# Cross-attention ahead of a product-key expert layer: 32-row and 32-column matmuls for scores and values, a transposed copy of x, softmax divided before the values, setup in one block with the attention

## The chip, the cores and the metric

The kernel runs on one core of one Trainium2 chip. The metric is the device time of one launch in microseconds (us), as the median of three runs; the profile is one further execution of the same program. The core has five engines with instruction queues of their own: TensorE (PE, matmuls; its weight loads are listed apart as PEld), VectorE (DVE), ScalarE (ACT), GpSimd (POOL) and SyncE (SP, which here only starts transfers).

## The reference, cut

```python
def _L0_xattn_ref(query, key, value, mask, wq, bq, wk, bk, wv, bv, wo, bo):   # H = 16, HD = 32
    q = query @ wq + bq; k = key @ wk + bk; v = value @ wv + bv
    score = jnp.einsum('bhqd,bhkd->bhqk', q, k) / jnp.sqrt(jnp.float32(HD))
    score = score + (1.0 - mask) * -1000000000.0
    alpha = jax.nn.softmax(score, axis=-1)
    context = jnp.einsum('bhqk,bhkd->bhqd', alpha, v)
    return context.transpose(0, 2, 1, 3).reshape(b, -1, D) @ wo + bo
...
x = x + _L0_xattn_ref(_layernorm(x), ctx_1024, ctx_1024, mask_Bx1x1xS2_ff1, ...)
x = x + _L0_ffn_ref(_layernorm(x), w_q, bn_gamma, bn_beta, keys, down_embed, up_embed)
```

x is 2 x 2048 x 512 in fp32, the context 2 x 77 x 512, so that each of 4096 tokens has 16 heads of 77 scores. The second line is a product-key layer: queries are normalised over the batch, the 8 best of 128 keys are taken twice for each of 8 heads, 64 rows of two tables of 16384 x 512 are fetched for each token, and they are weighted with gelu and softmax. Everything is fp32.

## The kernel before, in words

The tokens are 32 tiles (`NT`) of 128 (`P`), 16 to a batch. The program has three blocks, each ended by all engines.

`setup_block` loads the weights and makes what all tiles share: the keys, projected, as `kbd`, a matrix for each batch with the four heads of a group of 128 rows on its diagonal (`GK` = 308 columns for each of four groups, `KC`), and the values as `v_pack`, which holds for each of ten chunks of 128 (head, token) pairs (`NCH`) the 96 columns (`VW`) of the three heads that it can touch, with zeros elsewhere.

`attention_block` runs a pipeline over the tiles. In step s, TensorE works for tile s (it turns the normalised x, `turn_x`, projects the queries in four parts, `project`, and multiplies with `kbd`, `score`), for tile s-2 (it turns the exponentials into `probT`, `turn_prob`, multiplies with `v_pack`, `values`, and turns the sum, `turn_attention`) and for tile s-3 (`output`, the product with wo). `values` begins with a matmul of zeros that opens the whole bank. VectorE adds the mask and takes and subtracts the maximum (`shift_scores`), sums the exponentials (`sum_exp`), divides what the values gave (`norm_attention`), scales q (`scale_q`), normalises x (`norm_x`), and adds the residual with its statistics (`residual`). ScalarE takes one Exp over all 1232 scores and copies what TensorE turned out of PSUM. GpSimd makes the reciprocal roots, adds bo to a second load of x, and normalises x2. When the last tile's scores are done, `second_moments` (x2 transposed times x2, for the batch normalisation) fills TensorE for the rest of the block. What sets the order is the code: each engine's `step` is written out by hand, with semaphores between them.

`expert_block` makes the normalised scoring matrix and then, for each tile, fetches 64 rows for each token with indirect transfers (line 809), takes dot products on VectorE and ScalarE (lines 990 and 1173) and sums weighted rows on TensorE (line 1354).

An fp32 matmul stands in the trace as two records of TensorE, each with a weight load of its own; a transpose is one record. So the 16 matmuls of `project` for a tile are 32 records.

## Time and profile before

| | |
|---|---|
| median of three runs | 3672.28 us (3667.19 to 3675.46) |
| profiled execution, its own time | 3638.82 us |
| its span, first to last instruction | 3637.0 us |
| mean granted clock of TensorE | 0.919 |
| TensorE matmul, VectorE, ScalarE, GpSimd busy | 83%, 67%, 47%, 59% |
| end of the setup block | 27.0 us |
| end of the attention block | about 562 us |

The busy shares are means over three unlike stages. The setup and the attention take the first 562 us, the preparation of the experts some 130 us more, and the rest of the span is the loop over the experts' rows. The profiled execution was 33 us faster than the median of the runs.

### The profile page before, as it was taken

The page shows a single profiled execution, that of the slowest core. Times are in us where ns is not written, and L with a number is a line of the kernel's source. Part 1 is how long each engine was busy: PE and PEld are TensorE (multiplying, and loading weights), DVE is VectorE, ACT ScalarE, POOL GpSimd, SP SyncE. Part 2 cuts the span into 40 slices and gives each one's busy share as a digit, 9 for nine tenths or more (in the row PEclk, how much of TensorE's full clock was granted, in tenths as well). Part 3 has the DMA queues.
Part 4 walks back from the last instruction along what each step waited for, and adds up shares of the span by engine and source line. Part 5 has one row for each costly group of instructions (what it writes and reads, how often), then busy time and mean ns, then how long its engine had stood idle before and what let it go on. Part 6 is the DMA issues. An engine that isn't in the chain of part 4 may idle for free.

```text
span 3637.0 us, 33429 instructions
## 1 busy us (share of the span) xinstructions
PE 3004.5 (83%) x8862; PEld 1495.1 (41%) x8862; DVE 2429.0 (67%) x5214; ACT 1722.7 (47%) x5109; POOL 2134.2 (59%) x2225
## 2 busy tenths in 40 slices
PE   8999999787877877778888878878887877788777
PEld 6787866333333333333333333333333333333333
DVE  5777725576766766667766766667666666666665
ACT  1222201455554555555555555555554555555555
POOL 1343421466666666666666666666666666666665
PEclk9999999899999999988999989989998999999989
DMA  5111101799999999999999999999999999999997
GB/s 191 52 61 52 58 18 55 275 366 368 368 367 364 369 368 368 372 365 362 368 365 371 368 369 375 368 361 362 370 366 366 380 361 366 368 368 361 364 374 306
DMA packets 324684, 1132.59 MB, mean 311 GB/s; under 512 B 36187, under 2 KB 36827, under 8 KB 323880
## 3 DMA queue, kind: packets, MB, share of 16 engines
q0 software_dynamic: 294912, 1073.87, 77.1%
q1 hardware_dynamic: 28800, 55.92, 4.4%
q10 hardware_dynamic: 808, 0.99, 0.1%
q8 instruction: 56, 0.92, 0.1%
q14 instruction: 108, 0.88, 0.1%
HBM read 1113.87 MB, written 16.78 MB: 311 GB/s over the span
## 4 chain that ended last, share of the span: by engine, by line
ACT 23%; another core or an unknown queue 17%; DVE 16%; PE 14%; issue 14%; DVEq 0%; ACTq 0%
ACT rows L1173 16%; PE banks L1354 9%; DVE rows L990 5%; PE banks L1333 3%; DVE expert_diag L1004 3%; ACT expert_act_h L1185 2%; ACT expert_more_rows L1173 2%; DVE expert_top_s L905 2%; DVE expert_top_i L913 1%; PE banks L1268 1%; ACT L1185 1%; DVE expert_best_i L936 1%; DVE expert_coef L996 1%; ACT L1168 1%
## 5 line engine op out<-in xcount | busy, mean ns | idle before, releaser
L809 POOL DMA_INDIRECT rows<-in_table,expert_idx x1824 | 1729.2, 948 | 952.3 <-issue 642.4
L1354 PE MATMUL banks<-rows,expert_diag 128*128 128x512 f32 x3648 | 1753.2, 630 | 494.7 <-DVE expert_diag L1004 310.4
L1173 ACT ACTIVATE rows<-rows 128x512 f32<-128x512 f32 x1824 | 1123.7, 617 | 749.9 <-DVE expert_coef L996 386.6
L1354 PEld LDWEIGHTS banks<-rows,expert_diag 128*128 128x128 f32 x3648 | 719.5, 202 | 1482.2 <-issue 1010.8
L990 DVE TENSOR_TENSOR rows<-rows,banks 128x2048 f32<-128x2048 f32 x456 | 1037.2, 2275 | 11.9 <-issue 6.9
L996 DVE TENSOR_TENSOR expert_coef<-expert_act_h,expert_prob 128x4 f32<-128x4 f32 x512 | 80.6, 157 | 848.7 <-remote 500.6
L1333 PE MATMUL banks<-amat,expert_xnT 128*128 128x512 f32 x992 | 466.1, 592 | 7.8 <-issue 5.8
L1004 DVE TENSOR_TENSOR expert_diag<-banks,expert_coef 128x512 f32<-128x512 f32 x512 | 346.6, 677 | 29.5 <-remote 15.7
L1173 ACT ACTIVATION_READ_ACCUMULATOR rows<-rows 128x1 f32 x1824 | 340.5, 187 | 0.3
L1185 ACT ACTIVATE expert_act_h<-expert_hid 128x4 f32<-128x4 f32 x512 | 105.2, 205 | 437.5 <-remote 339.7
L1354 PE MATMUL banks<-expert_more_rows,expert_diag 128*128 128x512 f32 x448 | 225.7, 650 | 80.5 <-DVE expert_diag L1004 41.8
L1333 PEld LDWEIGHTS banks<-amat,expert_xnT 128*128 128x128 f32 x992 | 188.3, 190 | 243.4 <-issue 239.8
L809 POOL DMA_INDIRECT expert_more_rows<-in_table,expert_idx x224 | 212.1, 947 | 121.3 <-issue 88.6
L1173 ACT ACTIVATE expert_more_rows<-expert_more_rows 128x512 f32<-128x512 f32 x224 | 138.1, 617 | 84.6 <-DVE expert_coef L996 43.9
L1354 PEld LDWEIGHTS banks<-expert_more_rows,expert_diag 128*128 128x128 f32 x448 | 91.3, 209 | 208.2 <-issue 140.6
L373 POOL TENSOR_TENSOR rstd<-attention_var_eps,minus_half 128x1 f32<-128x1 f32 x32 | 17.9, 560 | 246.7 <-DVE attention_var_eps L460 246.7
L913 DVE FIND_INDEX8 expert_top_i<-expert_top_s,banks 128x8 uint32<-128x128 f32 x512 | 139.4, 288 | 20.5 <-issue 20.2
L586 PE MATMUL banks<-attention_xnT,amat 128*128 128x128 f32 x1024 | 137.3, 279 | 2.1 <-ACT attention_xnT L524 2.1
L586 PEld LDWEIGHTS banks<-attention_xnT,amat 128*128 128x128 f32 x1024 | 128.3, 194 | 16.8 <-issue 13.9
L990 DVE TENSOR_TENSOR expert_more_rows<-expert_more_rows,banks 128x2048 f32<-128x2048 f32 x56 | 127.4, 2275 | 0.8 <-issue 0.8
L905 DVE MAX8 expert_top_s<-banks 128x8 f32<-128x128 f32 x512 | 113.1, 282 | 9.8 <-PE banks L1333 8.0
L552 PE MATMUL banks<-amat,attention_attT 128*128 128x512 f32 x256 | 115.2, 592 | 0.0
(133 smaller groups left out, 2227.2 us busy)
## 6 DMA issues: line engine op xcount, KB each, us to landing
rows<-in_table,expert_idx POOLq DMA_INDIRECT x1824
x_t<-in_x SPq DMA_DIRECT2D x32, 256.0 KB, 2.9
attention_xr_t<-in_x SPq DMA_DIRECT2D x32, 256.0 KB, 2.8
x_dram<-rows SPq DMA_DIRECT2D x32, 256.0 KB, 2.0
expert_x_t<-x_dram SPq DMA_DIRECT2D x32, 256.0 KB
out_y<-expert_x_t SPq DMA_DIRECT2D x32, 256.0 KB
rows<-in_w_q SPq DMA_DIRECT2D x4, 1024.0 KB, 6.3
rows<-in_w_qT SPq DMA_DIRECT2D x4, 1024.0 KB, 8.5
```

Source lines behind the costliest of these rows:

```text
L552: mm = pe.matmul(att_ps[:, :], attT[:, c, :], attn_w[:, 1, c, :], start=(c == 0), stop=(c == KC - 1))
L586: mm = pe.matmul(q_ps[:, j, :], attn_w[:, 0, c, j * P:(j + 1) * P], xnT[:, c, :], start=(c == 0), stop=(c == KC - 1))
L809: pool.indirect_dma_start(four(n)[:, k, :], None, table[:, :], bass.IndirectOffsetOnAxis(ap=idx[:, t % 2, at:at + 1], axis=0))\
L905: ins = dve.max(top_s[:, m * TOP:(m + 1) * TOP], score_ps[:, q % 2, i * NK:(i + 1) * NK])
L913: ins = dve.max_index(top_i[:, h // HH, m % 2, h % HH, :], top_s[:, m * TOP:(m + 1) * TOP], score_ps[:, q % 2, i * NK:(i + 1) * NK])
L990: return dve.tensor_tensor(down, down, xn_ps[:, par, :].unsqueeze(1).to_broadcast([P, HALF, D]), ALU.mult)
L996: dve.tensor_tensor(coef[:, j % RING, :], act_h[:, j % RING, :], prob[:, par, j * HALF:(j + 1) * HALF], ALU.mult)\
L1004: dve.tensor_tensor(diag[:, j % RING, :, :], ident_ps.unsqueeze(1).to_broadcast([P, HALF, P]), coef[:, j % RING, :].unsqueeze(2).to_broadc ...
L1173: ins = act.activation(down, down, ACT.Copy, accum_out=hid[:, j % RING, k:k + 1])
L1185: act.activation(act_h[:, j % RING, :], hid[:, j % RING, :], ACT.Gelu_apprx_tanh)\
L1333: mm = pe.matmul(score_ps[:, q % 2, :], xnT[:, par, c, :], amat[:, c, q * 512:(q + 1) * 512], start=False, stop=(c == KC - 1), skip_group_ ...
L1354: mm = pe.matmul(out_ps[:, par, :], diag[:, j % RING, k, :], four(t * HALVES + j)[:, k, D:2 * D], start=(j == 0 and k == 0), stop=(j == HA ...
```

## The change

It touches the first two blocks and one input; `expert_block` is the same text. Setup and attention become one block. The host also hands over x transposed by tile (`x_T`), so that x is neither normalised nor turned ahead of the projection: the mean is taken out of wq once (`centre`), and the reciprocal root of the variance multiplies the scores instead. The bias of q becomes a bias of the scores (`score_bias`, made once for each batch, with the mask in it). Scores are 16 matmuls of 32 rows (one for each head, `scores_of`), and those of the heads r, r+4, r+8, r+12 lie in bank r. Values are 25 matmuls whose stationary side is 32 columns of `v_pack` and whose moving side is a chunk of `probT`; head h writes rows 32 (h mod 4) and following, so the result is already turned. For that, the softmax is divided before it is turned (`normalize`, in two halves), and the maximum is subtracted as the bias of 16 Exp instructions, one for each head. `output` is cut in two around `score`. All loops are written out.

```diff
+            def load_xT(t):
+                wait(sp, "q_done", t - XT_RING + 1)
+                sp.dma_start(xT_t[:, t % XT_RING], x_T[t]).then_inc(xT_in[t % XT_RING], 16)
...
-            def shift_scores(m, par, batch):
...
-                wait(dve, "probT_turned", (m - 1) * NG)
...
-                for i, (h0, n) in enumerate(SCORE_HEADS):
-                    ins = dve.tensor_tensor(
-                        prob[:, par, h0:h0 + n, :],
-                        score_ps[:, i, 0:n * SK].rearrange("p (h k) -> p h k", h=n),
-                        mb.unsqueeze(1).to_broadcast([P, n, SK]), ALU.add)
-                ins.then_inc(ev["masked"], 1)
-                wait(dve, "masked", m + 1)
-                dve.tensor_reduce(smax[:, :], prob[:, par], AX.X, ALU.max).then_inc(ev["max_done"], 1)
-                wait(dve, "max_done", m + 1)
-                dve.tensor_tensor(prob[:, par], prob[:, par],
-                                  smax[:, :].unsqueeze(2).to_broadcast([P, H, SK]),
-                                  ALU.subtract).then_inc(ev["shifted"], 1)
...
+            def mask_scores(t):
+                b = t // TPB
+                to, bias = by_row(prob[:, t % 2]), by_row(score_bias[b])
+                dve.wait_ge(ev["score_done"], t + 1)
+                dve.wait_ge(ev["rstd_done"], t + 1)
+                dve.wait_ge(ev["bias_kept"], (b + 1) * G)
+                wait(dve, "probT_turned", (t - 1) * NG)
+                for r in range(G):
+                    dve.scalar_tensor_tensor(out=to[r], in0=score_bank(0, r), scalar=rstd[:, t:t + 1],
+                                             in1=bias[r], op0=ALU.mult, op1=ALU.add)\
+                       .then_inc(ev["masked"], 1)
+                dve.wait_ge(ev["masked"], (t + 1) * G)
+                dve.tensor_reduce(neg_max[:, t % 2, :], prob[:, t % 2], AX.X, ALU.max, negate=True)\
+                   .then_inc(ev["max_done"], 1)
+            def normalize(t, half):
+                n = 2 * t + half
+                some = slice(half * H // 2, (half + 1) * H // 2)
+                dve.wait_ge(ev["exp_done"], n + 1)
+                dve.tensor_reduce(ssum[:, t % 2, some], prob[:, t % 2, some], AX.X, ALU.add)\
+                   .then_inc(ev["sum_done"], 1)
+                dve.wait_ge(ev["sum_done"], n + 1)
+                dve.reciprocal(rsum[:, t % 2, some], ssum[:, t % 2, some]).then_inc(ev["rsum_done"], 1)
+                dve.wait_ge(ev["rsum_done"], n + 1)
+                dve.tensor_tensor(prob[:, t % 2, some], prob[:, t % 2, some],
+                                  rsum[:, t % 2, some].unsqueeze(2).to_broadcast([P, H // 2, SK]),
+                                  ALU.mult).then_inc(ev["normed"], 1)
...
+            def exps(t, heads):
+                for h in heads:
+                    ins = act.activation(prob[:, t % 2, h, :], prob[:, t % 2, h, :], ACT.Exp,
+                                         bias=neg_max[:, t % 2, h:h + 1])
+                    if h % (H // 2) == H // 2 - 1:
+                        ins.then_inc(ev["exp_done"], 1)
...
+            def copy_attT(b):
+                act.wait_ge(ev["att_part"], (b + 1) * NG)
+                wait(act, "wo_done", b)
+                act.activation(attT[:, :, :], att_ps, ACT.Copy).then_inc(ev["attT_done"], 1)
...
+            for s in range(NT + 1):
+                now, back = s < NT, s >= 1
+                if back:
                     copy_probT(s - 1, 0)
-            pipeline(act, step)
+                    copy_probT(s - 1, 1)
+                if now:
+                    act.wait_ge(ev["max_done"], s + 1)
+                    exps(s, range(0, 8))
+                if back:
+                    copy_probT(s - 1, 2)
+                if now:
+                    exps(s, range(8, 12))
+                if back:
+                    copy_attT(s - 1)
+                if now:
+                    exps(s, range(12, 14))
+                if s + 1 < NT:
+                    copy_qT(s + 1)
+                if now:
+                    exps(s, range(14, 16))
...
-            def turn_x(t):
-                wait(pe, "xn_done", t + 1)
-                wait(pe, "attT_done", t - 2)
-                for c in range(KC):
-                    mm = pe.transpose(turn_ps[:, c, :], xn_t[:, c * P:(c + 1) * P], ident[:, :])
-                mm.then_inc(ev["xn_turned"], 1)
...
+            def scores_of(first, queries, b):
+                for g in range(KC):
+                    for r in range(G):
+                        rows = slice(r * HD, (r + 1) * HD)
+                        mm = pe.matmul(score_bank(first, r)[:, g, :], queries[rows, g, :],
+                                       k_sb[rows, g, b * SK:(b + 1) * SK], start=True, stop=True)
+                return mm
+            def project(t, js):
+                for j in js:
+                    if j == 0:
+                        pe.wait_ge(xT_in[t % XT_RING], (t // XT_RING + 1) * 16)
+                        wait(pe, "masked", (t - 1) * G + 1)
+                    for c in range(KC):
+                        mm = pe.matmul(banks[:, Q_BANK, j * P:(j + 1) * P],
+                                       attn_w[:, 0, c, j * P:(j + 1) * P], xT_t[:, t % XT_RING, c, :],
+                                       start=(c == 0), stop=(c == KC - 1))
+                    if j == KC - 1:
+                        mm.then_inc(ev["q_done"], 1)
+            def score(t):
+                pe.wait_ge(ev["qT_done"], t + 1)
+                wait(pe, "masked", t * G)
+                scores_of(0, qT, t // TPB).then_inc(ev["score_done"], 1)
...
-            def values(b, r, batch):
+            def values(b, r):
 
                 if r == 0:
-                    if isinstance(b, int) and b == 0:
-                        wait(pe, "zeros_made", 1)
+                    wait(pe, "attT_done", b)
+                pe.wait_ge(ev["probT_done"], b * NG + r + 1)
+                pairs = [(c, h) for c in CHUNK_GROUPS[r] for h in range(H)
+                         if h * SK < (c + 1) * P and (h + 1) * SK > c * P]
+                for c, h in pairs:
+                    g, q = divmod(h, G)
+                    at = (h - FIRST_HEAD[c]) * HD
+                    mm = pe.matmul(att_ps[q * HD:(q + 1) * HD, g, :],
+                                   v_pack[:, b // TPB, c, at:at + HD],
+                                   probT[:, r, c % 4 * P:(c % 4 + 1) * P],
+                                   start=(c == h * SK // P), stop=(c == ((h + 1) * SK - 1) // P))
+                mm.then_inc(ev["att_part"], 1)
+            def output(b, cs):
+                if 0 in cs:
+                    pe.wait_ge(ev["attT_done"], b + 1)
                     wait(pe, "x2_done", b)
-                    pe.matmul(att_ps[:, :], zeros[:, 0:P], zeros[:, :], start=True, stop=False)
-                wait(pe, "probT_done", b * NG + r + 1)
-                for i, c in enumerate(CHUNK_GROUPS[r]):
-                    head0 = FIRST_HEAD[c] * HD
-                    mm = pe.matmul(att_ps[:, head0:head0 + VW], probT[:, r, i * P:(i + 1) * P],
-                                   v_pack[:, batch, c, :],
-                                   start=False, stop=(c == NCH - 1))
-                mm.then_inc(ev["att_part"], 1)
...
-            def score(t, batch):
-                wait(pe, "qT_done", t + 1)
-                wait(pe, "masked", t)
-                for i, (h0, n) in enumerate(SCORE_HEADS):
-                    h = h0
-                    while h < h0 + n:
-                        g, stop = h // G, min(h0 + n, (h // G + 1) * G)
-                        mm = pe.matmul(score_ps[:, i, (h - h0) * SK:(stop - h0) * SK], qT[:, g, :],
-                                       kbd[batch][:, g, (h - g * G) * SK:(stop - g * G) * SK],
-                                       start=True, stop=True)
-                        h = stop
-                mm.then_inc(ev["score_done"], 1)
...
-            def step(s, par, half, has, batch):
-                draining = isinstance(s, int) and s >= NT
-                now, back2 = 0 in has, -2 in has
-                if now:
-                    turn_x(s)
-                if -3 in has:
-                    output(s - 3)
-                if now:
-                    project(s, 0)
-                if back2:
-                    turn_prob(s - 2, par, 1)
-                if now:
-                    project(s, 1)
-                if back2:
-                    values(s - 2, 0, batch(-2))
-                    turn_prob(s - 2, par, 2)
-                if now:
-                    project(s, 2)
-                if back2:
-                    values(s - 2, 1, batch(-2))
-                    values(s - 2, 2, batch(-2))
-                if now:
-                    project(s, 3)
-                if draining and s < NT + 2:
-                    second_moments(2, first=(s == NT))
-                if back2:
-                    turn_attention(s - 2)
-                if draining and s < NT + 2:
-                    second_moments(2)
-                if -1 in has:
-                    turn_prob(s - 1, 1 - par, 0)
...
+                                   ctx_sb[:, c, :], start=(c == 0), stop=(c == KC - 1))
+                mm.then_inc(ev["k_made"], 1)
+            pe.wait_ge(ev["centre_made"], 1)
+            pe.wait_ge(wq_in, 16)
+            for c in range(KC):
+                mm = pe.matmul(banks[:, Q_BANK, :], centre[:, :], attn_w[:, 0, c, :],
+                               start=(c == 0), stop=(c == KC - 1))
+            mm.then_inc(ev["mean_made"], 1)
+            pe.wait_ge(ev["bq_spread"], 1)
+            pe.wait_ge(ev["k_biased"], KC)
+            scores_of(4, bq_wide, 0).then_inc(ev["bias_done"], 1)
+            pe.wait_ge(ev["centred"], KC)
+            project(0, range(KC))
+            score(0)
+            pe.wait_ge(ev["bias_kept"], G)
+            scores_of(4, bq_wide, 1).then_inc(ev["bias_done"], 1)
+            setup_values()
+            for s in range(NT + 2):
+                if s >= 2:
+                    output(s - 2, (2, 3))
+                if s == NT:
+                    second_moments(3)
+                if 1 <= s <= NT:
+                    if s == 1:
+                        pe.wait_ge(ev["pad_made"], 1)
+                        pe.wait_ge(ev["pack_kept"], len(PACK_BANKS))
...
+                    turn_prob(s - 1, 1)
+                if s + 1 < NT:
+                    project(s + 1, (0, 1, 2))
+                if s in (NT - 1, NT):
+                    second_moments(1)
+                if 1 <= s <= NT:
+                    turn_prob(s - 1, 2)
+                    for r in range(NG):
+                        values(s - 1, r)
+                if s + 1 < NT:
+                    project(s + 1, (3,))
+                if s in (NT - 1, NT):
+                    second_moments(1)
+                if 1 <= s <= NT:
+                    output(s - 1, (0, 1))
+                if s + 1 < NT:
+                    score(s + 1)
             second_moments(len(moments_left) - 1)
...
```

TensorE's own order shows what stands in one step of a tile. Here are the last twelve of the sixteen pieces of one step before, from after `output` to the scores; L546 `turn_x` (4 transposes) and L552 `output` (4 matmuls) stand ahead of them. L586 is `project`, L562 `turn_prob`, L572 the zeros, L576 `values`, L594 `turn_attention`, L605 `score`; the numbers are those of the output and the count.

```order
L586 MATMUL banks<-attention_xnT,amat 128x128 x4
L562 MATMUL banks<-ident,attention_prob_pad 128x128 x4
L586 MATMUL banks<-attention_xnT,amat 128x128 x4
L572 MATMUL banks<-attention_zeros 128x512
L576 MATMUL banks<-amat,attention_probT 128x96 x4
L562 MATMUL banks<-ident,attention_prob_pad 128x128 x2
L586 MATMUL banks<-attention_xnT,amat 128x128 x4
L576 MATMUL banks<-amat,attention_probT 128x96 x6
L586 MATMUL banks<-attention_xnT,amat 128x128 x4
L594 MATMUL banks<-ident,attention_att 128x128 x4
L562 MATMUL banks<-ident,attention_prob_pad 128x128 x4
L605 MATMUL banks<-bias_row,attention_qT 128x308
```

After that row come two of 128x154 and two more of 128x308, the rest of `score`. And a whole step of the changed kernel, in which L510 is `turn_prob`, L495 `project`, L524 `values`, L535 `output`, L485 `scores_of`.

```order
L510 MATMUL banks<-ident,attention_prob_pad 128x128 x8
L495 MATMUL banks<-attention_xT_t,amat 128x128 x12
L510 MATMUL banks<-ident,attention_prob_pad 128x128 x2
L524 MATMUL banks<-attention_probT,amat 32x128 x25
L495 MATMUL banks<-attention_xT_t,amat 128x128 x4
L535 MATMUL banks<-amat 128x512 x2
L485 MATMUL banks<-bias_row 128x77 x16
L535 MATMUL banks<-amat 128x512 x2
```

The two groups of four transposes (x and the attention) and the matmul of zeros are gone; ten matmuls of 96 columns are 25 with 32 columns of weights, and five of 154 or 308 columns are 16 of 77.

ScalarE before, in one step (L524 copies the turned x, L527 is Exp, L516 and L534 are copies of `probT` and `attT`):

```order
L524 ACTIVATE attention_xnT<-banks 128x512
L527 ACTIVATE attention_prob_pad<-attention_prob_pad 128x1232
L516 ACTIVATE attention_probT<-banks 128x512
L516 ACTIVATE attention_probT<-banks 128x256
L534 ACTIVATE attention_attT<-banks 128x512
L516 ACTIVATE attention_probT<-banks 128x512
```

And after (L433 is Exp of one head, L442 and L448 the same two copies, L428 the copy of the queries, which VectorE made before):

```order
L442 ACTIVATE attention_probT<-banks 128x512 x2
L433 ACTIVATE attention_prob_pad<-attention_prob_pad,attention_neg_max 128x77 x8
L442 ACTIVATE attention_probT<-banks 128x256
L433 ACTIVATE attention_prob_pad<-attention_prob_pad,attention_neg_max 128x77 x4
L448 ACTIVATE amat<-banks 128x512
L433 ACTIVATE attention_prob_pad<-attention_prob_pad,attention_neg_max 128x77 x2
L428 ACTIVATE bias_row<-banks 128x512
L433 ACTIVATE attention_prob_pad<-attention_prob_pad,attention_neg_max 128x77 x2
```

The last two heads' Exp now stands behind the copy of the next tile's queries, which waits for TensorE.

## Rows read from the trace of the kernel before

**Rows 1.** The page's first part: engine, busy us, share of the span, instructions.

```profile
PE 3004.5 (83%) x8862; PEld 1495.1 (41%) x8862; DVE 2429.0 (67%) x5214; ACT 1722.7 (47%) x5109; POOL 2134.2 (59%) x2225
```

**Rows 2.** Busy time by stretch: from:to, length, engines, granted clock, DMA share, GB/s.

```profile
200.00:300.00 100.00, 100.00 (x643) 79.84 (x642) 77.28 (x129) 27.55 (x44) 41.23 (x37) 1.00 0.17 56
...
690.00:3637.00 2947.00, 2364.78 (x5168) 1006.70 (x5168) 2009.80 (x4356) 1571.63 (x4846) 1906.93 (x2012) 0.91 0.95 364
```

**Rows 3.** TensorE's instructions over one step: start us, length us, engine, line.

```profile
259.58 0.60 PE L546 MATMUL banks<-ident,attention_xn_t 128*128 128x128 f32 x4
260.02 3.60 PE L552 MATMUL banks<-amat,attention_attT 128*128 128x512 f32 x8
263.45 1.05 PE L586 MATMUL banks<-attention_xnT,amat 128*128 128x128 f32 x8
264.34 0.60 PE L562 MATMUL banks<-ident,attention_prob_pad 128*128 128x128 f32 x4
264.78 1.06 PE L586 MATMUL banks<-attention_xnT,amat 128*128 128x128 f32 x8
265.77 0.38 PE L572 MATMUL banks<-attention_zeros 1*128 1x512 bf16 x1
266.08 1.13 PE L576 MATMUL banks<-amat,attention_probT 128*128 128x96 f32 x8
267.05 0.38 PE L562 MATMUL banks<-ident,attention_prob_pad 128*128 128x128 f32 x2
267.27 1.06 PE L586 MATMUL banks<-attention_xnT,amat 128*128 128x128 f32 x8
268.16 1.48 PE L576 MATMUL banks<-amat,attention_probT 128*128 128x96 f32 x12
269.48 1.08 PE L586 MATMUL banks<-attention_xnT,amat 128*128 128x128 f32 x8
270.42 0.66 PE L594 MATMUL banks<-ident,attention_att 128*128 128x128 f32 x4
270.92 0.60 PE L562 MATMUL banks<-ident,attention_prob_pad 128*128 128x128 f32 x4
271.35 2.34 PE L605 MATMUL banks<-amat,attention_qT 128*128 128x308 f32 x10
273.53 0.60 PE L546 MATMUL banks<-ident,attention_xn_t 128*128 128x128 f32 x4
```

**Rows 4.** TensorE's weight loads in the first 60 us, grouped: busy us, mean ns.

```profile
L219 PEld LDWEIGHTS setup_k_ps<-setup_v_sb,setup_repeat 77*128 77x128 f32 x40 | 4.6, 192 | 0.5 <-issue 0.5
...
L206 PEld LDWEIGHTS setup_v_ps<-amat,setup_ctx_sb 128*77 128x77 f32 x16 | 2.3, 147 | 4.1 <-issue 3.9
```

**Rows 5.** VectorE in the same step: start us, length us.

```profile
259.78 1.57 DVE L432 TENSOR_TENSOR attention_prob_pad<-banks,mask_bias 128x462 f32<-128x462 f32 x3 [1.78 <-PE banks L605]
...
262.86 1.44 DVE L440 TENSOR_TENSOR attention_prob_pad<-attention_prob_pad,attention_smax 128x1232 f32<-128x1232 f32 x1
264.22 0.68 DVE L449 TENSOR_TENSOR rows<-banks,attention_xr_t 128x512 f32<-128x512 f32 x1
...
268.82 0.25 DVE L484 RECIPROCAL attention_rsum<-attention_ssum 128x16 f32<-128x16 f32 x1
```

**Rows 6.** ScalarE's one Exp in the same step: start us, length us.

```profile
264.33 1.23 ACT L527 ACTIVATE attention_prob_pad<-attention_prob_pad 128x1232 f32<-128x1232 f32 x1 [3.52 <-DVE attention_prob_pad L440]
```

**Rows 7.** The page's groups of two other ScalarE instructions: busy us, mean ns.

```profile
L1173 ACT ACTIVATE rows<-rows 128x512 f32<-128x512 f32 x1824 | 1123.7, 617 | 749.9 <-DVE expert_coef L996 386.6
...
L1185 ACT ACTIVATE expert_act_h<-expert_hid 128x4 f32<-128x4 f32 x512 | 105.2, 205 | 437.5 <-remote 339.7
```

**Rows 8.** TensorE in the setup and at the second tile's scores: start us, length us.

```profile
14.53 7.09 PE L206 MATMUL setup_v_ps<-amat,setup_ctx_sb 128*77 128x512 f32 x16
...
21.45 4.60 PE L219 MATMUL setup_k_ps<-setup_v_sb,setup_repeat 77*128 77x96 f32 x40
...
48.69 3.79 PE L605 MATMUL banks<-bias_row,attention_qT 128*128 128x308 f32 x10 [1.65 <-DVE attention_qT L476]
```

648 lines of the change are left out of this document (288 added, 360 removed).

## The prediction, made before the changed kernel had run

> **What bounds the kernel now.** The first thing to read is the busy share by stretch [rows 2]. In the loop over the experts' rows the transfer engines are busy 95% of the time, and no edit touches that loop. In the attention TensorE is busy 100.00 of 100 us at the full clock (1.00, 2.4 GHz), VectorE 77.3, ScalarE 27.6, GpSimd 41.2, and the transfers take 0.17. So the attention is TensorE's, and the 83% that the page gives for the whole [rows 1] hides this. The second view is TensorE's timeline over one step [rows 3]: turn_x starts at 259.58 and again at 273.53, so that a tile costs 13.95 us, with no hole between the groups. Taken from start to start, the step is: turn_x 0.44, output 3.43, project 0.89 + 0.99 + 0.89 + 0.94, turn_prob 0.44 + 0.22 + 0.43, the zeros 0.31, values 0.97 + 1.32, turn_attention 0.50, score 2.18. What the change is worth is what it does to this sum, 31 times (the first tile's front is made in the setup), until VectorE or the chain through ScalarE is longer.
>
> **What goes.** turn_x 0.44, the zeros 0.31, values 2.29, turn_attention 0.50, score 2.18. The project ahead of the zeros lasts 0.99 where its like takes 0.89, and the zeros' 0.31 is 0.10 over half of the 0.43 that one 512-column record of output takes (3.43 / 8): the one instruction with a single row of weights costs about 0.10 before and 0.10 behind it [rows 3]. So 5.82 us go and 8.13 stay: output, project and turn_prob, whose shapes don't change.
>
> **What comes, in records.** An fp32 matmul is two records. A record with 128 weight columns takes 0.111 us when it moves 128 columns (0.89 / 8) and still 0.110 when it moves 96 (1.32 / 12) [rows 3]: below 128 moved columns the load or the issue sets the pace. The scores are 16 matmuls, 32 records with 128 weight columns and 77 moved: alone, 0.11 each, 3.52 us where 2.18 were. The values are 25 matmuls, 50 records with 32 weight columns and 128 moved; the load is lighter (147 ns with 77 columns, 192 with 128 [rows 4]), the moved side not: alone, 0.11 each, 5.5 us where 2.29 were. Scores use one 32-row strip of the array, values one 32-column strip, each step of the loops takes another strip, and scores go to four banks. Everything hangs on how many strips work at once, and no row of this trace shows two instructions in different strips. The bounds, from the 0.11:
> - One at a time: 3.52 + 5.5 = 9.0 us.
> - Two abreast, in the order of issue. The two records of one matmul share a strip, so only the second of one and the first of the next overlap. Scores: 16 x 0.11 = 1.76. Values: nine heads cross a chunk's edge and follow themselves in their own strip, so 15 of the 24 changes overlap: 50 - 15 = 35 records, 3.85. Together 5.6.
> - Four abreast: the fullest values strip has 7 matmuls, 1.54; scores 8 records to a strip, 0.88. Together 2.4.
>
> To each comes the switch into and out of strips, twice in a step: 4 x 0.10 = 0.4, priced by the single-row instruction [rows 3].
>
> I take about three abreast: 32 / 3 x 0.11 = 1.17, 50 / 3 x 0.11 = 1.83, and 0.5 for the nine heads that follow themselves, 3.5 in all. Nothing in the rows picks this depth; it lies between the bounds, nearer the low one because the loops rotate over all four strips. The step is then 8.13 + 0.4 + 3.5 = 12.0 us, 1.95 less, 31 times: 60 us. The step breaks even at 5.4 for scores and values together, a little under two abreast.
>
> The trace cannot say whether strips overlap. The Trainium skill can ("TensorE: Matmul & The Clock Gate", Part 3): it gives 3.07 times for four row tiles and 2.38 times for three column tiles, at 512 moved columns. By these, as an estimate, 3.52 / 3.07 + 5.5 / 2.38 = 3.5 us, the value taken above. No run here shows it yet. The same part has the rule that speaks against the change: matmuls start in program order, and only weight loads are pulled ahead; that is the second rival.
>
> **VectorE.** It is busy 10.8 us a step (77.3 / 100 x 13.95 [rows 2, 3]). It loses the subtraction of the maximum (1.44 [rows 5]), the division of the values and the scaling of q (512 elements, as the residual's 0.68 [rows 5]), the normalising of x (priced as the same) and a small copy, together some 3.6. It gains the division of 1232 probabilities in two halves (1.44 by the row of the same size, plus a start of 0.1), a second sum and reciprocal (about 0.3) and a fourth piece of the masking (1.57 for three [rows 5], 0.1 for one more): 2.0. About 9.2 us are left, 10 with its own waits, under 12.0.
>
> **ScalarE.** One Exp of 1.23 us [rows 6] becomes 16 with 77 elements. Between 205 ns for 4 elements and 617 for 512 [rows 7] that is 0.26 each, 4.2 us. It was busy 3.8 us a step (27.55 x 0.1395 [rows 2]) and comes to 6.8; the copy of q takes the place of that of x. The chain that matters: scores, mask and maximum 3.1, eight Exp 2.1, the third copy of probT 0.4, the last group of values about 0.6, the last part of project 0.9, half of output 1.7, next scores 1.3: 10.1 us, hidden under 12.0 and bare if TensorE needed less. The last two Exp stand behind the copy of q, which waits for project; after it come 0.6 + 0.5 on ScalarE and 1.8 for the second division on VectorE, while TensorE has half of output and the scores (3.0) and only then, behind the other half (1.7), turns the probabilities. Slack of over 1 us.
>
> **Setup.** Before, the second tile's scores end at 48.69 + 3.79 = 52.5 [rows 8]. After, from the end of the keys' projection at 14.5 (where the next group starts [rows 8]): the mean of wq, 8 records, 3.4; four VectorE passes over wq at 0.7, 2.8; project 3.7; copy 0.7; scores 1.4; mask and maximum 3.1 and the second batch's bias 1.7, for which TensorE waits; values' projection 7.1; bias 0.7; packing 4.6 [rows 8]; project, copy and scores 5.8: 49.5. That is 3 us won, with the block's barrier gone in it. The second moments, GpSimd's work and the moved transfers (0.17 of the engines' time [rows 2]) are costed at nothing: the moments are the same work on TensorE, GpSimd has 59 of 100 us free, and x_T comes three tiles ahead. Without that cover a load of x_T would cost its landing once a tile.
>
> **The sum.** The profiled execution took 3638.8 us: less 60 and 3 it is 3576. The median of the runs shown lies 33.5 higher, at 3672.3, since the profiled execution was a quick one; less 63 it is **3609**, given as 3610.
>
> **Rivals.**
> - Four abreast: the step is 10.95, TensorE and the chain of 10.1 are near each other; 3.0 x 31 + 3 = 96 off, 3576. Chance 0.17, against 0.40 for the forecast, whose own range is 3585 to 3650.
> - Two abreast. A matmul's two records are in one strip, so an engine that starts them in order cannot look past the second: the step is 8.53 + 5.6 = 14.15, 0.2 x 31 = 6 more, 3 less from the setup: 3675, no change. Chance 0.18.
> - Weight loads decide (the other side). If the scores' loads, each 128 columns, don't overlap though the matmuls do, scores stay at 3.52 and with values at 3.85 the step is 15.9: 60 - 3 = 57 more, 3729. It costs from 5.4 us for both on. The rows bear this out as far as they go: at 96 moved columns a record still took 0.110. Chance 0.13. The skill's page, section "LDWEIGHTS (loading the stationary operand)", says that a load of 32 rows takes as long as one of 128, by columns; the trace agrees on the columns (147 against 192 ns).
> - No overlap at all: the step is 17.5, 3.6 x 31 - 3 = 109 more, 3781. Chance 0.10: then the change doesn't do what its strips are for.
> - A rest of 0.02 for a bound that I don't see.
>
> Faster: 0.40 + 0.17 and a part of two abreast, 0.60. The same within 0.2% (7 us, about what a measurement of this kernel can tell from no change): 0.13. Slower: 0.27. The range leaves out the case without overlap and reaches from just under four abreast over the weight loads' case: 3565 to 3735.
>
> **What would show it.** In TensorE's timeline after: values' group 1.5 to 2.5 us long from start to start is right, 3.9 is two abreast, 5.5 is none; scores' group 0.9 to 1.3, 1.8 or 3.5. The step from scores to scores should be 12.0 with TensorE busy throughout and the granted clock at 1.00; VectorE's share should be under 85%. If the step is shorter than the groups on TensorE allow, my 8.13 is wrong; if it is longer and TensorE waits, it is the chain through the 16 Exp. Second scores past 55 us would make the setup wrong. The loop over experts must not differ by more than its own spread.

## The result and the profile after

The changed kernel takes 3585.69 us (3580.72 to 3588.9, 4 runs) where the kernel before took 3672.42 (3667.19 to 3675.46): a ratio of 0.9764, 95% interval 0.9746 to 0.9782, 86.7 us less. A second comparison gave 3559.5 against 3647.6 us, ratio 0.9757 (0.9743 to 0.9771), 88.1 less, with the same step of 11.26 us. The forecast was 3610, 62 less, with 3565 to 3735 as its range. The direction and the place were right, the size too small: 3585.7 stands at the edge of the forecast's own range (3585 to 3650), and nearer to the rival of four abreast (3576) than to the forecast. What was expected of the second comparison, once the first was known:

> The changed kernel once more, unaltered, as the measure for the three beside it. Every theory expects the ratio 0.976 to the kernel before, within 0.002, and a step of 11.26 us.

The page's first part, as [rows 1]:

```profile
PE 2962.2 (83%) x10310; PEld 1431.4 (40%) x10310; DVE 2389.8 (67%) x5220; ACT 1815.7 (51%) x5589; POOL 2142.7 (60%) x2224
```

It says almost nothing: 42 us of TensorE in 3000. The busy shares by stretch, the columns of [rows 2], say where to look.

```profile
8.60:27.00 18.40, 16.02 (x104) 13.28 (x104) 6.68 (x16) 0.00 (x0) 1.82 (x2) 0.91 1.04 395
27.00:52.50 25.50, 20.02 (x164) 13.38 (x168) 12.26 (x21) 5.24 (x18) 1.80 (x2) 0.87 0.40 156
...
200.00:300.00 100.00, 100.00 (x1156) 75.91 (x1155) 82.34 (x161) 60.54 (x189) 54.82 (x45) 1.00 0.23 73
```

TensorE is still busy 100 of 100 us at the full clock, with nearly twice the records (1156 for 643). VectorE rose from 77 to 82%, ScalarE from 28 to 61%. One step of the attention on TensorE (start us, length us), the counterpart of [rows 3]:

```profile
241.91 1.88 PE L535 MATMUL banks<-amat 128*128 128x512 f32 x4
243.72 1.13 PE L485 MATMUL banks<-bias_row 32*128 32x77 f32 x32
244.78 1.98 PE L535 MATMUL banks<-amat 128*128 128x512 f32 x4
246.60 1.04 PE L510 MATMUL banks<-ident,attention_prob_pad 128*128 128x128 f32 x8
247.48 2.84 PE L495 MATMUL banks<-attention_xT_t,amat 128*128 128x128 f32 x24
250.16 0.38 PE L510 MATMUL banks<-ident,attention_prob_pad 128*128 128x128 f32 x2
250.47 1.78 PE L524 MATMUL banks<-attention_probT,amat 128*32 128x128 f32 x50
252.17 1.16 PE L495 MATMUL banks<-attention_xT_t,amat 128*128 128x128 f32 x8
253.17 1.88 PE L535 MATMUL banks<-amat 128*128 128x512 f32 x4
```

A step is 253.17 - 241.91 = 11.26 us where it was 13.95. The scores (L485) hold 1.06 us from start to start where they were 2.18 [rows 3], the values (L524) 1.70 where they were 2.29 and had 0.81 of zeros and transposes beside them. Fifty records of 128 columns in 1.70 us are 0.034 each: alone each needs 0.109, so that more than three were under way at a time. The starts of single records say the same for the scores: the 32 start in eight bursts of four, 7 ns apart inside a burst and 0.11 us from burst to burst (0.17 behind the first); their weight loads come in the same bursts.

Where the 86.7 us are: 31 x 2.69 = 83.4 in the steps. From the start to the experts' first matmul the profiled executions went from 561.8 to 477.0 us, 84.8 less: the steps, 0.7 lost in the setup, and a rest of 2, which is put down to the filling and emptying of the pipeline. The rest of the difference lies inside what two sets of runs vary by. The loop over the experts' rows is no part of it; it varied on its own. These rows are the kernel before and the changed one, from the first weighted row to the end:

```profile
693.60:3637.00 2943.40, 2364.75 (x5168) 1006.66 (x5168) 2007.09 (x4351) 1568.29 (x4838) 1906.93 (x2012) 0.91 0.95 364
```

```profile
611.20:3586.60 2975.40, 2405.63 (x5168) 1022.65 (x5168) 2011.94 (x4351) 1568.03 (x4838) 1904.94 (x2012) 0.90 0.95 360
```

The same 5168 records took 32 us more in the changed kernel's profiled execution. Spans of two single executions therefore show 50 us of difference where the runs show 87, and only the part ahead of the loop can be compared between traces.

### The profile page after: what moved, and what is told of

Read it like the earlier page. It is cut to its first block, busy times and chain, and to the rows that moved or that the text cites. A ratio compares the mean times of both kernels' runs of the same rounds, so it can differ in the third digit from the quotient of the medians.

```text
span 3586.6 us, 36078 instructions
## 1 busy us (share of the span) xinstructions
PE 2962.2 (83%) x10310; PEld 1431.4 (40%) x10310; DVE 2389.8 (67%) x5220; ACT 1815.7 (51%) x5589; POOL 2142.7 (60%) x2224
## 4 chain that ended last, share of the span: by engine, by line
another core or an unknown queue 19%; PE 18%; ACT 18%; DVE 18%; issue 13%; DVEq 0%; ACTq 0%
PE banks L1321 13%; ACT rows L1140 12%; DVE rows L957 6%; PE banks L1300 4%; DVE expert_diag L971 4%; DVE expert_top_s L872 2%; ACT expert_more_rows L1140 2%; ACT expert_act_h L1152 2%; DVE expert_top_i L880 1%; PE banks L1235 1%; DVE expert_coef L963 1%; DVE expert_more_rows L957 1%; DVE expert_best_i L903 1%; ACT L1152 1%
## 5 line engine op out<-in xcount | busy, mean ns | idle before, releaser
L1321 PE MATMUL banks<-rows,expert_diag 128*128 128x512 f32 x3648 | 1793.4, 642 | 476.4 <-DVE expert_diag L971 203.8
L1321 PEld LDWEIGHTS banks<-rows,expert_diag 128*128 128x128 f32 x3648 | 734.7, 206 | 1485.6 <-issue 1096.9
L433 ACT ACTIVATE attention_prob_pad<-attention_prob_pad,attention_neg_max 128x77 f32<-128x77 f32 x512 | 140.4, 347 | 8.6 <-DVE attention_neg_max L338 6.6
L255 POOL TENSOR_TENSOR attention_rstd<-attention_var_eps,minus_half 128x1 f32<-128x1 f32 x32 | 17.9, 559 | 205.4 <-DVE attention_var_eps L314 205.4
L495 PE MATMUL banks<-attention_xT_t,amat 128*128 128x128 f32 x1024 | 129.4, 280 | 1.5 <-DVE amat L403 1.5
L495 PEld LDWEIGHTS banks<-attention_xT_t,amat 128*128 128x128 f32 x1024 | 120.7, 194 | 7.7 <-issue 6.0
L535 PE MATMUL banks<-amat 128*128 128x512 f32 x256 | 123.2, 605 | 0.0
```

The costliest lines, as they stand in the source:

```text
L433: ins = act.activation(prob[:, t % 2, h, :], prob[:, t % 2, h, :], ACT.Exp, bias=neg_max[:, t % 2, h:h + 1])
L495: mm = pe.matmul(banks[:, Q_BANK, j * P:(j + 1) * P], attn_w[:, 0, c, j * P:(j + 1) * P], xT_t[:, t % XT_RING, c, :], start=(c == 0), stop ...
L535: mm = pe.matmul(out_ps, attT[:, c, :], attn_w[:, 1, c, :], start=(c == 0), stop=(c == KC - 1))
L1321: mm = pe.matmul(out_ps[:, par, :], diag[:, j % RING, k, :], four(t * HALVES + j)[:, k, D:2 * D], start=(j == 0 and k == 0), stop=(j == HA ...
```

## The experiments

### Is it the strips? Values in one strip, scores in one strip

```diff
-                    mm = pe.matmul(att_ps[q * HD:(q + 1) * HD, g, :],
+                    mm = pe.matmul(att_ps[0:HD, g, :],
```

> All heads' values are written to rows 0 to 31 of the bank (strip 0), so that the context of most heads is left out; the bank is cleared once before. Same matmuls, same order. This prices the overlap of the values' strips: if it is the strips that make them cheap, the group takes 50 x 0.109 = 5.5 us in place of 1.7, the step 15.0, 3.75 x 32 = 120 more, 3706. Rival (the 32-column weights alone make them cheap, whatever the strip): the group stays near 1.7 and the time at 3586.

Measured: ratio 1.011 (1.0093 to 1.0127), 3703.9 us against 3664.6. The step is 15.13 us. In the timeline the values' group is L526:

```profile
252.86 5.65 PE L526 MATMUL banks<-attention_probT,amat 128*32 128x128 f32 x50
258.44 1.16 PE L497 MATMUL banks<-attention_xT_t,amat 128*128 128x128 f32 x8
```

(The view ends at 260 us; the group is whole.) It takes 5.58 us from start to start, 50 x 0.109 and the switch. So the overlap of strips is worth 3.88 us a step, 120 us of the kernel; without it the change would have lost.

```diff
-                        rows = slice(r * HD, (r + 1) * HD)
+                        rows = slice(0, HD)
```

> All score matmuls read rows 0 to 31 of queries and keys (strip 0), so that the scores are those of other heads; banks and order as they were. If strips overlap in both the loads and the matmuls, taking that away costs 32 x 0.111 = 3.55 us in place of 1.06, 2.5 x 32 = 80 more, 3666. Rival (in one strip the 128-column loads still hide and the 77 moved columns decide): 32 x 0.067 = 2.1 us, 34 more, 3620.

Measured: ratio 1.0145 (1.0124 to 1.0166), 3716.9 us, which is 140 more than the changed kernel's ratio of 0.976 would give. That is 60 us more than the first theory said and some hundred more than the rival. The group:

```profile
242.80 4.64 PE L485 MATMUL banks<-bias_row 32*128 32x77 f32 x32
247.37 3.78 PE L535 MATMUL banks<-amat 128*128 128x512 f32 x4
250.94 1.74 PE L510 MATMUL banks<-ident,attention_prob_pad 128*128 128x128 f32 x8
```

In the steps that ran at full clock it takes 3.72 us, 32 x 0.111 and the switches, as expected: with one strip it isn't the 77 moved columns that set the pace. Whether it is the 128-column load or a least time of a record is not shown: in one strip the values' records, with 32 weight columns and 128 moved, take 0.109 as well. The banks still rotate here as in the changed kernel, so that it is the strips that overlap, not the banks. But here it takes 4.57, and the four records of output behind it 3.57 in place of 1.82. The busy shares by stretch show why (the granted clock is the third number from the end):

```profile
240.00:247.00 7.00, 7.00 (x45) 5.76 (x44) 1.97 (x4) 2.16 (x6) 3.39 (x2) 0.90 0.01 2
247.40:251.00 3.60, 3.60 (x6) 1.43 (x6) 3.31 (x5) 0.00 (x0) 0.00 (x0) 0.50 0.00 0
```

TensorE had been busy the whole time, and the clock fell to 1.2 GHz all the same; what it had done before it fell was to work 32 rows of the array at a time. In the changed kernel, with the same number of instructions over four strips, the clock is 1.00 in every step. Two parts make 135 of the 140 us: 2.66 x 31 = 82 for the longer groups, and about 116 us at half speed up to 515 us, 106 more than the changed kernel has, which cost half of that, 53.

### Does the order of issue matter?

Scores strip after strip, four matmuls (eight records) to each:

```diff
-                for g in range(KC):
-                    for r in range(G):
+                for r in range(G):
+                    for g in range(KC):
```

> The 16 score matmuls of a tile are issued strip after strip (four of strip 0, then four of strip 1, and so on) in place of rotating; nothing else changes. In the changed kernel the scores' group takes 1.06 us from start to start, in bursts of four records. Theory A (each strip of the array takes its records from a common window whatever their order): the group stays at about 1.1 us, the step at 11.26, the time at 3586 within 0.2%. Theory B (records start in program order, and rotating is what makes strips overlap): only the three changes of strip overlap, 32 x 0.111 - 3 x 0.111 = 3.2 us, the step 13.4, 2.1 x 32 = 68 us more, 3654.

Measured: ratio 0.997 (0.9957 to 0.9984), 3651.5 us. The group (the row behind it is cut off by the view's end):

```profile
252.91 2.65 PE L485 MATMUL banks<-bias_row 32*128 32x77 f32 x32
255.49 1.10 PE L535 MATMUL banks<-amat 128*128 128x512 f32 x1
```

2.58 us, between the 1.06 of theory A and the 3.2 of B. The step is 12.78 at full clock, and the clock was 0.93 over the attention (58 us at half speed, where the changed kernel has 10, in its setup): that is the rest of the loss. The time lies by theory B's 3654 by chance: the group cost less than B said, and the clock made up for it. The group is now longer than the old shape's 2.18 [rows 3], and 13 us are left of the whole change's 87, by the order of two loops alone. The starts of single records show where a strip holds up the next: strip 0's start at 240.134, .305, .417, .528 and .640, and the first that goes into another strip at 240.646, behind the fifth of eight; the two changes that follow, at 241.158 and 241.669, look the same. (The strip isn't named in the trace; the first record into an idle strip is the one that takes 329 ns, the others 270.)

Values sorted by strip inside each group, two or three matmuls to a strip:

```diff
+                pairs.sort(key=lambda pair: (pair[1] % G, pair[1], pair[0]))
```

> Within each of the three groups of a tile, the value matmuls are sorted by strip. Theory A (order doesn't matter): the values' group stays at 1.7 us, 3586. Theory B (program order decides): a strip's records follow each other, at most the changes of strip overlap; 50 x 0.109 less 10 changes gives 4.4 us in place of 1.7, 2.7 x 32 = 86 more, 3672, which is the time of the kernel before.

Measured: ratio 0.9809 (0.9792 to 0.9825), 3594.7 us, the step 11.71 us.

```profile
245.57 2.23 PE L525 MATMUL banks<-attention_probT,amat 128*32 128x128 f32 x50
247.73 1.16 PE L495 MATMUL banks<-attention_xT_t,amat 128*128 128x128 f32 x8
```

2.16 us, 0.45 more than in turn: near theory A, not at it. So neither theory held for both, and the difference between the two was the length of a run in one strip: eight records against four to six. Hence a third:

```diff
-                for g in range(KC):
-                    for r in range(G):
+                for g, r in [(gg + i, r) for gg in (0, 2) for r in range(G) for i in range(2)]:
+                    if True:
```

> Scores issued two matmuls (four records) to a strip before the next strip, twice round. With one to a strip the group takes 1.06 us, with four to a strip 2.58. Theory A (TensorE looks a fixed few records ahead of the oldest that waits): about two strips at once most of the time, 1.6 to 1.9 us, a step 0.6 to 0.8 longer, 19 to 25 us more than the changed kernel, ratio 0.981 to 0.983. Theory B (each strip holds a short list of its own, of four records): four strips at once, 1.06 us, ratio 0.976.

```profile
244.86 1.21 PE L485 MATMUL banks<-bias_row 32*128 32x77 f32 x32
245.99 1.98 PE L535 MATMUL banks<-amat 128*128 128x512 f32 x4
```

1.13 us against 1.06, the step 11.33. The ratio is 0.9754 (0.974 to 0.9767), 3238.6 us, 81.5 below the kernel before on a chip where that takes 3320; since the loop is shorter there, the ratio can't be laid beside the 0.976, and the step decides. Theory B holds as far as it was tried: a run of four records to a strip costs 0.07 us, a run of eight 1.5. A window of fixed length over the whole order, as theory A has it, cannot give that: with two by two, the first record of the fourth strip stands twelve behind the first of the first strip, and a window that long would have reached the second strip at once in the order strip after strip. That each strip has a short list of its own, and that a full list stops all behind it, is what fits all three, and the fifth of eight in the starts above puts its length at about four records, one of them at work. The list itself is in no row.

### The old shape of the values, beside the new scores

```diff
+                if r == 0:
+                    pe.matmul(banks[:, ATT_BANK, :], zeros[:, 0:P], zeros[:, :], start=True, stop=False)
+                for c in CHUNK_GROUPS[r]:
+                    head0 = FIRST_HEAD[c] * HD
+                    mm = pe.matmul(banks[:, ATT_BANK, head0:head0 + VW],
+                                   probT[:, r, c % 4 * P:(c % 4 + 1) * P],
+                                   v_pack[:, b // TPB, c, :], start=False, stop=(c == NCH - 1))
...
+            def turn_attention(b):
+                pe.wait_ge(ev["att_kept"], b + 1)
+                for c in range(KC):
+                    mm = pe.transpose(att_ps[:, c, :], att[:, c * P:(c + 1) * P], ident[:, :])
```

> The changed kernel with the values in the old shape: a matmul of zeros, ten matmuls with probT as weights and 96 moved columns, a copy to SBUF on ScalarE, four transposes back, and then the copy to attT; x is kept in 6 buffers in place of 8, for space. Scores and all else stay. Theory A (TensorE's work alone): the strips' values cost 1.90 us of the step with their switches; the old shape costs 0.41 for the zeros, 2.2 for 20 records and 0.5 for the transposes, 3.1: step 12.45, 37 us more than the changed kernel, ratio 0.986. Theory B (what the new shape wins is the shorter way through ScalarE): the second copy stands bare ahead of output, the step is 12.9 or more and the time 50 us more or above, ratio 0.990.

Measured: ratio 0.9907 (0.9891 to 0.9922), 3289.4 us, 30.8 below the kernel before; the step is 12.92. One stall stands ahead of the scores, in brackets:

```profile
254.42 0.60 PE L543 MATMUL banks<-ident,attention_att 128*128 128x128 f32 x4
255.33 0.91 PE L495 MATMUL banks<-bias_row 32*128 32x77 f32 x24 [0.31 <-ACT bias_row L431]
```

Theory B's size, but the wait is another: TensorE waits for the copy of the queries, which ScalarE makes behind the copy of the values, not for the turned values ahead of output. Of the 2.69 us that the change wins in a step, 1.66 are the values' (13.95 less the changed kernel's 11.26 is 2.69; 12.92 less 11.26 is 1.66), 1.3 of them TensorE's own work and the rest this wait; the scores and the turning of x make up the other 1.0. Read off the groups, with their switches and without this wait, the values win 1.30, the scores 0.93 and the turning of x 0.44; the last two were not taken apart by a run.

### Do the 16 Exp cost or give anything?

```diff
+                dve.tensor_tensor(prob[:, t % 2], prob[:, t % 2],
+                                  neg_max[:, t % 2, :].unsqueeze(2).to_broadcast([P, H, SK]),
+                                  ALU.add).then_inc(ev["max_done"], 1)
...
+                if heads[0] == 0:
+                    act.activation(prob[:, t % 2], prob[:, t % 2], ACT.Exp).then_inc(ev["exp_done"], 2)
```

> VectorE adds the negated maximum over all 1232 scores again and ScalarE takes one Exp, in place of 16 with a bias; the rest of the changed kernel stays. In the changed kernel VectorE waits 1.6 us a step for the last two Exp and is otherwise at work or in its own waits for 9.6 of 11.26 us. Theory A (TensorE alone bounds the step, the 16 Exp cost nothing): the pass adds 1.44 + 0.07, the wait goes, VectorE's chain is 11.15, a step of 11.26 still, the same time within 0.2%. Theory B (the 16 Exp are what makes room, VectorE is next at once): the small waits at the Exp and at the copies add up to more than the 0.1 left, the step is 11.6 to 12.2, 10 to 30 us more.

Measured: ratio 0.9763 (0.9749 to 0.9776), beside 0.9757 of the changed kernel in the same runs; the step is 11.26 again.

```profile
100.00:200.00 100.00, 100.00 (x1181) 76.10 (x1180) 95.26 (x170) 33.69 (x54) 59.03 (x45) 1.00 0.22 73
```

VectorE is at 95% and ScalarE at 34%, TensorE at 100%: theory A. The long way through ScalarE was hidden, and the pass that it replaces would have been too: VectorE still has 5% of the time idle. The changed kernel's own waits (who waited for what: us in total over 300 us, times, longest) show the slack that this used up:

```profile
DVE attention_ssum L346 <- ACT attention_prob_pad L433: 43.7, 28, 1.6
```

### The setup, and an order with one switch fewer

```diff
+                if s == 0:
+                    keep_bias(1)
                 if s < NT:
                     mask_scores(s)
                 if s == 0:
-                    keep_bias(1)
                     pack_values()
```

> In the setup VectorE makes the second batch's score bias ahead of masking the first tile, in place of behind it. In the changed kernel TensorE stands 4.1 us before the projection of the values, for this bias. Theory A (that wait is the setup's loss): it shrinks to about 2 us and the second tile's scores end 2 us earlier, 51 in place of 53.2; 2 us in the total, below what the runs can tell. Theory B (the loss is the clock, half speed for 6.8 us behind the wait): it goes with the wait, and the scores end 3 to 4 us earlier. Rival: the first tile's softmax is late in turn, TensorE waits before turning it, and nothing is won.

Measured: ratio 0.9747 (0.9734 to 0.976), 3554.4 us beside the changed kernel's 3559.5. The setup on TensorE, first the changed kernel's, then this one's:

```profile
21.53 5.46 PE L495 MATMUL banks<-attention_xT_t,amat 128*128 128x128 f32 x32 [1.51 <-DVE amat L403]
27.68 1.13 PE L485 MATMUL banks<-bias_row 32*128 32x77 f32 x32 [0.69 <-ACT bias_row L428]
...
33.82 9.56 PE L560 MATMUL banks<-amat,rows 128*77 128x512 f32 x16 [4.12 <-DVE amat L323]
...
52.11 1.13 PE L485 MATMUL banks<-bias_row 32*128 32x77 f32 x32 [0.69 <-ACT bias_row L428]
```

```profile
31.01 7.09 PE L561 MATMUL banks<-amat,rows 128*77 128x512 f32 x16 [1.75 <-DVE amat L323]
...
46.83 1.13 PE L486 MATMUL banks<-bias_row 32*128 32x77 f32 x32 [0.69 <-ACT bias_row L429]
```

The wait fell from 4.12 to 1.75 us, and here the projection of the values behind it kept the full clock: 7.09 as in [rows 8], where it had been 9.56. The second scores end at 47.9 in place of 53.2 (50.9 in the changed kernel's second profile). The clock's part is not sure: in the profiles of the kernel with both edits, below, the wait was 1.76 and the projection 8.79. Theory A with some of B; the rival's wait didn't come.

```diff
-                    output(s - 2, (2, 3))
...
-                    project(s + 1, (0, 1, 2))
+                    project(s + 1, range(KC))
...
-                if s + 1 < NT:
-                    project(s + 1, (3,))
...
-                    output(s - 1, (0, 1))
                 if s + 1 < NT:
                     score(s + 1)
+                if 1 <= s <= NT:
+                    output(s - 1, range(KC))
```

> An order of TensorE's step with one change of tiling fewer: all of project, then values, the next scores right behind them, then output in one piece; ScalarE copies the queries earlier and the turned values last. The changed kernel pays about 0.1 us into and 0.2 out of each strip group. Theory A (TensorE's work alone bounds the step, and the switch is paid between full and strip tiles): the step falls by 0.15 to 0.3 us, 5 to 9 us in all. Theory B (a switch between rows and columns costs as much as two): no change. Rival on the other side: the second division on VectorE ends later, or output waits for the last copy, and the step grows to 11.5 or more, 8 us or more in all.

Measured: ratio 0.9744 (0.973 to 0.9757), 3553.8 us (3551.5 to 3554.1) beside 3559.5 (3552.8 to 3562.5) for the changed kernel in the same runs.

```profile
248.91 1.77 PE L522 MATMUL banks<-attention_probT,amat 128*32 128x128 f32 x50
250.61 1.13 PE L483 MATMUL banks<-bias_row 32*128 32x77 f32 x32
251.68 2.84 PE L533 MATMUL banks<-amat 128*128 128x512 f32 x6
```

(The last row is cut off by the view's end.) The two strip groups are as long as they were. What is saved is behind the values and ahead of the scores, where full tiles had stood: all of project takes 3.58 us where its two pieces took 3.68, and output 3.54 for 3.63. The step is 11.06: 0.20 less, theory A. VectorE is at 92%.

> The two edits that made the changed kernel quicker together: scores right behind values, and the second batch's score bias ahead of the first mask. If they add, the step is 11.06 us and the second scores end near 48: 9 us less than the changed kernel, ratio 0.9735. If the late second division on VectorE eats the setup's gain, 0.9745.

Measured: ratio 0.9722 (0.9709 to 0.9735), 3228.0 us against 3320.2, 92.1 less.

> The kernel with both edits once more, unaltered, because its first comparison fell where the kernel before took 3320 us, against 3648 for the changed kernel's. If the edits add, it is 92 to 97 us below the kernel before wherever it runs, as in the first comparison, where the changed kernel was 86.7 and 88.1 below; if 92 was chance, 86 to 88.

Measured: ratio 0.9739 (0.9723 to 0.9755), 3546.5 us against 3642.8, 96.3 less. The step is 11.06 in both, and the experts' first matmul stands at 467.0 and 467.8 us (474.7 and 477.0 in the changed kernel's profiles). The second scores end at 47.5 and 48.3 us. Both gains are there in the traces. In the runs 92.1 and 96.3 less stand beside 86.7 and 88.1 for the changed kernel, about 7 us more on the mean, though no comparison has both kernels; it is the quickest version here, though the intervals of the ratios of changed kernel and this one still touch.

## Why the prediction came out as it did

- **What bounds it**: right. TensorE was at 100% before and is after, and no wait stands between its groups.
- **What goes, 5.82 us, and what stays, 8.13**: right. The groups that stay take 8.50 from start to start (1.81 + 1.82 + 0.88 + 2.68 + 0.31 + 1.00), of which 0.37 are switches beside the strip groups, so that 8.13 is what they took before.
- **Three abreast, 3.5 us for scores and values**: this is the term that was mis-sized. Start to start and without the switches they take 0.95 and 1.61, 2.56 in all; the bound for four abreast was 2.4. 0.94 us less a step is 29 us in 31 steps. The next term, the switches, took 0.17 x 31 = 5.3 us of that back, the setup 3.7 (0.7 lost for 3 won), and the rest of 2 is the pipeline's ends: 62 + 29 - 5.3 - 3.7 + 2 is 84, beside the 84.8 measured ahead of the experts. The rival "four abreast" had the mechanism, with a chance of 0.17. Nothing in the trace of before chose between the depths, as the prediction said, so that three was a guess between bounds, and that the time fell into the wide range says little for it. Its signs could not have told three from four either: 1.5 to 2.5 us for the values and 0.9 to 1.3 for the scores hold both. The scores strip after strip and two by two show what sets the depth.
- **The switches, 0.4 us from the single row of zeros**: 0.57. The way in costs 0.1, as there, the way out 0.2, because the first record behind a strip group is late and the second again.
- **Records alone at 0.11**: right, 3.72 us with switches for the scores in one strip, 5.58 for the values.
- **Two abreast, from starting in order**: false. The rule of the Trainium skill on which it leaned ("TensorE: Matmul & The Clock Gate", Part 3, matmuls in program order) would give 1.76 us for the scores, and at least 25 record times, 2.8 us, for two by two; the trace has 0.95 (1.06 with the switch) and, with the switch, 1.13. The 3.07 times that the same part of the Trainium skill gives for four row tiles is nearer: 3.55 / 0.95 is 3.7 here.
- **Weight loads decide**: false across strips. 32 loads of 128 columns fit into 0.95 us, so that those of different strips overlap too. Within a strip they may decide: 0.111 a record with 77 moved columns is not the moved side, but a least time of 0.11 a record would look the same.
- **VectorE 9.2 us a step, 10 with its waits**: 9.27 (82.34 x 0.1126), and 9.6 with waits. **ScalarE 6.8**: 6.8.
- **The chain through the Exp, 10.1 us, hidden**: it was hidden, and with one Exp in place of the 16 the step didn't change.
- **Setup, 3 us won**: 0.7 lost in one profile, 1.6 won in the other. From the first scores to the projection of the values, where TensorE waits for the bias, it was 5.2 us for the 4.8 forecast. What the sum left out was the clock, 0.91 over 8.6 to 27 us and 0.87 over 27 to 52.5: the first projection of queries took 5.46 us, 1.7 more than the next of its kind, and the projection of the values 9.56, 2.5 more than in [rows 8]. Another 0.9 was a wait for the load of wq, which the second profile doesn't have.

## What to carry to other kernels

Matmuls that use a quarter of the array are worth their larger number only if the order of issue keeps all four strips supplied: two or four records to a strip in turn ran nearly four abreast, eight in a row lost most of it, and one strip alone lost all, and for 32-row strips the clock too. Price such a change from the strip with the most records at the rate of one record alone, add 0.1 us into and 0.2 out of each group of strips, and place strip groups next to each other. When TensorE is at 100% ahead of a loop that varies by 30 us between executions, compare the traces up to the loop, and take the whole from runs.

## What the runs showed that was not expected

The clock of TensorE fell while it was busy without a gap: 0.88 to 0.91 over the attention with the scores in one strip, 0.93 with the scores strip after strip, 1.00 with the same instructions in turn. In the traces of the kernel before and of the changed one every fall up to the experts stood behind a pause of TensorE. It is not any single strip that does it: with the values in one 32-column strip, 5.6 us at a time, the clock stayed at 1.00 through the attention. The stretch from 200 to 300 us, first of the run with the values in one strip, then of the one with the scores:

```profile
200.00:300.00 100.00, 100.00 (x880) 81.91 (x879) 64.39 (x126) 45.24 (x142) 37.94 (x33) 1.00 0.17 56
```

```profile
200.00:300.00 100.00, 100.00 (x825) 78.50 (x824) 59.71 (x113) 40.04 (x126) 39.28 (x32) 0.88 0.15 49
```

Whether the number of rows at work (32 for those scores, 128 for these values) makes the difference, or something else, no run shows.

The same programs ran a tenth faster in one comparison: 3320 us for the kernel before, where others had 3643 to 3672. All of it is behind the attention. The two profiles of the kernel with both edits (3225.1 and 3544.5 us) reach the experts at 467.0 and 467.8 us and the first weighted row at 574.1 and 599.6: 25 us of the difference lie in the preparation, some 294 in the loop. The loop with two by two, from its first weighted row to the end:

```profile
586.20:3238.80 2652.60, 2322.54 (x5168) 974.63 (x5168) 2030.49 (x4351) 1572.62 (x4838) 1903.53 (x2014) 0.97 1.01 405
```

The transfers moved 405 GB/s where they moved 360 to 364 elsewhere; the attention's step of the kernel with both edits was 11.06 in both places. Differences in us carry over from one comparison to another within some 4 us, as 92.1 and 96.3 did; ratios shift with the loop.
